# A step's score maxima turned into eight rows a head by one matmul, copied once by ACT and spread over the diagonal blocks by POOL, one step ahead

## The chip, the cores and the metric

The kernel runs on one core of one Trainium2 chip. The metric is the device time of one execution in microseconds. Its engines are TensorE (PE), VectorE (DVE), ScalarE (ACT), GpSimd (POOL) and SyncE (SP, which only issues transfers here). Each runs its own program in order and waits on semaphores.

## What is computed

A decoder layer on x of 8 x 128 tokens x 128 features, in fp32. Cut to what matters:

```
x = x + attn(layernorm(x))            # self-attention, 16 heads of 8; q and k pass a convolution;
                                      # scores = q.k / sqrt(8) * tau + delta, then softmax
x = x + xattn(layernorm(x), ctx, mask)# cross-attention, 16 heads of 8, keys from ctx, masked
x = x + ffn(layernorm(x))             # 64 experts, 8 of them chosen by a router, and a shared one
```

Both softmaxes are taken over 128 keys, with the row's maximum subtracted.

## The kernel before

The attention part has 16 steps: step s works on batch b = s % 8 of layer n = s // 8. The 16 heads are held as four groups g of four heads j. Partition block j (32 rows) of a "stacked" tile holds head 4g+j in column group g: high, middle and low parts of an fp32r split of its 8 features (from rows S_HI, S_MID, S_LO on), and in rows 0 and 1 of the block the constant ones (keys) or nothing (queries). `stack` on TensorE makes such tiles with selection matrices `pick`, ACT (`stacked_keys`, with the bias `ones_rows`) and DVE copy them to `kst` and `qst`.

For each step and group there are two products of scores:

- `scores(s, g)`: queries by a block-diagonal `kbd` (written by eight transfers a step from SP), tokens on the partitions. DVE's `maximum` reduces it over the keys to `rawmax`, negated. These scores serve for the maxima alone.
- `scoresT(s, g)`: `kst` by the block-diagonal `qbd`, keys on the partitions. `qbd` holds the queries and, in rows 0 and 1 of each 32-row block, high and low part of the negated maximum, so that the product already has the maximum subtracted. ACT's `exponential` reads it, `pv` multiplies by the values and a column of ones, `copy_o`, `turn_out`, `norm`, `turn_on`, `copy_on`, `project` and `add_residual` finish the batch, with the statistics of the next layer norm behind them (`stats_of`).

In the second layer each product of scores is preceded by a bf16 product that adds the mask.

How `qbd` comes about (before): DVE's `split_max(s)` writes the maxima as columns 32j and 32j+1 of a 128x4x128 tile `negmax` (one 128-column block for each g, fp32, the rest zero). TensorE's `turn_max(s)` (lines 482 to 492) puts the stacked queries into `bank[5]` by an identity product and adds four 128-column fp32 transposes of `negmax`, one for each g. Then ACT copies the 32-row blocks j = 0, 1 to the diagonal blocks of `qbd` (line 855, two instructions, `qbd_high`) and DVE j = 2, 3 (line 1098, two, `qbd_ready`).

The order of each engine's work is written out by hand in the loop over s. TensorE, plain step: `scores(s+1,0)`, `turn_max(s)`, `scores(s+1,1)`, `project(s-2)`, `pv(s-1,0)`, `pv(s-1,1)`, `scores(s+1,2)`, `pv(s-1,2)`, `pv(s-1,3)`, `scoresT(s,0)`, `scoresT(s,1)`, `scores(s+1,3)`, `turn_out(s-1)`, `scoresT(s,2)`, `scoresT(s,3)`, `turn_on(s-1)`. `later(s, place)` puts the stacking of queries and keys and the second layer's values, for which there was no time before, at places 0 to 3 of steps 0 to 5. Steps 7 and 11 (`making`) make the second layer's stacked queries and have their `scores(s+1, ...)` late in the step. ACT, plain step: the two copies, `copy_o(s-1)`, four `exponential`s, `copy_on(s-1)`. DVE: `split_max(s)`, `maximum(s+1,0)`, its two copies, `maximum(s+1,1)`, `add_residual(s-2)`, `maximum(s+1,2)`, `maximum(s+1,3)`, `norm(s-1)`.

POOL has little in the steps: it scales the first layer's values (line 1371), it runs `normalise` (lines 246 to 267: 15 linked operations on 128x4, then four of 128x128) and `add_bias` (line 272) for each half of the batches once the statistics of residuals 0 to 3 (DVE step 5) and 4 to 7 (step 9) are there, it splits the first three pairs of expert weights (lines 1398 to 1405), and then runs `normalise` for the third layer norm's first half (residual 11, step 13). The expert stage behind the attention, some 160 us, is not touched.

Of the kernel before, what the change touches and what calls it, by code (L numbers as in the profile page):

```python
# [15 lines left out]
P = 128  # L16
B = 8
# [12 lines left out]
S_HI, S_MID, S_LO = 2, 2 + DK, 2 + 2 * DK  # L30
# [26 lines left out]
def decoder_layer(nc, x, ctxT, mask, pack_a, pack_b, w3, rowsd, outT):  # L57
# [3 lines left out]
    with ExitStack() as ctx:  # L61
# [3 lines left out]
        def sem(name):  # L65
# [49 lines left out]
        negmax = sb("negmax", [P, G, P])  # L115
# [84 lines left out]
        (scored, maxed, max_split, max_turned, qbd_high, qbd_ready, scoredT, exped, pv_done, o_copied, o_turned, normed,  # L200
         on_turned, on_copied, projected, residual) = (sem(n) for n in (
             "scored", "maxed", "max_split", "max_turned", "qbd_high", "qbd_ready", "scoredT", "exped", "pv_done", "o_copied",
# [148 lines left out]
        def _(pe):  # L351
# [142 lines left out]

            def scoresT(s, g):
                n, b = s // B, s % B
                i = G * s + g
                if g == 0:
                    pe.wait_ge(qbd_high, s + 1)
# [71 lines left out]
            scores(0, 3)  # L571
            for s in range(STEPS + 1):
# [29 lines left out]
                if s >= 1:  # L602
                    pv(s - 1, 0)
                    pv(s - 1, 1)
                    if early:
                        scores(s + 1, 2)
# [4 lines left out]
                elif early:  # L611
                    scores(s + 1, 2)
# [4 lines left out]
                if early:  # L617
                    scores(s + 1, 3)
# [6 lines left out]
                if now:  # L625
                    scoresT(s, 2)
                if making is not None:
# [7 lines left out]
                if making is not None:  # L635
                    turn_out(s - 1)
                if making is not None:
# [7 lines left out]
                if 1 <= s < STEPS:  # L645
                    turn_on(s - 1)

# [97 lines left out]
        def _(act):  # L745
# [38 lines left out]
            def stacked_keys(n, c, g, b=7):  # L784
                act.wait_ge(k_stacked, G * (2 * n + c) + g + 1)
                act.activation(half(kst[n][:, g, :, :], c), four(b), ACT.Identity,
                               bias=A("ones_rows")).then_inc(kst_ready, 1)
# [105 lines left out]

            for s in range(STEPS + 1):
# [33 lines left out]
                if s >= 1:  # L928
                    copy_on(s - 1)

# [44 lines left out]
        def _(dve):  # L975
# [45 lines left out]

            for m, at in ((0, S_HI), (0, S_LO), (1, S_MID), (2, S_HI), (2, S_MID), (3, S_LO)):
# [62 lines left out]
            def split_max(s):  # L1085
                dve.wait_ge(maxed, G * s + G)
                wait(dve, max_turned, s)
                cols = negmax[:, :, :].rearrange("p g (j c) -> p g j c", j=J)
                link(dve.tensor_copy(cols[:, :, :, 0:1].bitcast(F32R), rawmax[:, s % 2, :, :].unsqueeze(3)))
                dve.tensor_tensor(cols[:, :, :, 1:2], rawmax[:, s % 2, :, :].unsqueeze(3), cols[:, :, :, 0:1],  # L1090
                                  ALU.subtract).then_inc(max_split, 1)

            def queries_with_max(s):
# [382 lines left out]
```

## Time and profile before

| what | value |
|---|---|
| time, median of 3 runs | 351.7 us (349.95 to 353.64) |
| span of the profiled execution | 351.6 us (that run's own time 353.76) |
| PE busy | 321.5 us (91%) |
| DVE busy | 273.0 us (78%) |
| ACT busy | 219.1 us (62%) |
| POOL busy | 171.6 us (49%) |
| share of PE in the chain that ended last | 63% |

Busy time counts a matmul from its start to its modelled end, so overlapping matmuls show an engine as full that still waits a little. The granted clock is TensorE's, in tenths of full speed on the page and as a fraction elsewhere. A row "x2" in a timeline is two like instructions one after the other, and the bracket behind a row is the idle time before it with what ended it. The span runs from 0; the attention steps lie between 50 and 175 us.

### The profile page before, as it was taken

Reading aid. Unit: us, or ns where it says so; the run is one execution under the profiler, and the core shown is the slowest. Engines: PE = TensorE matmul, PEld = TensorE weight load, DVE = VectorE, ACT = ScalarE, POOL = GpSimd, SP = SyncE. Lnnn points to the kernel's source line nnn. Section 1 sums busy time; section 2 is a strip of 40 time slices with the busy share of each in tenths; the row PEclk is TensorE's granted clock in tenths of the full one; section 3 lists DMA queues with packets and bytes.
Section 4 is the critical chain, followed back from the end, with each engine's and each line's share of the span. In section 5 each row is a group of like instructions: output and inputs, shape, how many; then the busy total and the mean of one; then the engine's idle time right before and its main releaser. Section 6 shows DMA issues by size and latency. Waiting matters only on the chain.

```text
span 351.6 us, 6529 instructions
## 1 busy us (share of the span) xinstructions
PE 321.5 (91%) x1874; PEld 225.4 (64%) x1874; DVE 273.0 (78%) x580; ACT 219.1 (62%) x457; POOL 171.6 (49%) x247
## 2 busy tenths in 40 slices
PE   1799978999999999999965999799989999999995
PEld 1544855777666676666753676566667777777773
DVE  4997766678886777787798969999996666777664
ACT  1287724866786457456744696567667676667763
POOL 9430010000080039107148787677777677777772
PEclk9999966999999999999998999999999999999999
DMA  7600110121120121121000123133223233222201
GB/s 289 209 1 0 23 31 7 32 61 32 30 50 16 39 53 33 23 51 56 2 2 0 30 71 103 47 90 89 74 66 97 81 90 90 80 82 86 67 1 62
DMA packets 20971, 20.58 MB, mean 59 GB/s; under 512 B 3152, under 2 KB 20304, under 8 KB 20816
## 3 DMA queue, kind: packets, MB, share of 16 engines
q1 hardware_dynamic: 20944, 20.25, 21.0%
q8 instruction: 13, 0.21, 0.3%
q14 instruction: 14, 0.11, 0.1%
HBM read 15.78 MB, written 0.52 MB: 46 GB/s over the span
## 4 chain that ended last, share of the span: by engine, by line
PE 63%; DVE 13%; POOL 11%; issue 9%; ACT 2%; DMA 1%; POOLq 0%; ACTq 0%; DVEq 0%
PE bank L356 41%; POOL qbd L1418 7%; PE bank L491 5%; PE bank L731 3%; PE bank L733 3%; PE bank L732 3%; PE bank L716 2%; PE bank L504 2%; PE bank L478 2%; POOL kst L1393 2%; DVE rawmax L1082 1%; DMA xres<-x 1%; PE bank L522 1%; DVE qbd L1098 1%; POOL xn L266 1%
## 5 line engine op out<-in xcount | busy, mean ns | idle before, releaser
L356 PE MATMUL bank<-khl,kst 128*128 128x512 f32 x396 | 105.2, 401 | 3.4 <-DVE kst L1119 3.0
L1418 POOL TENSOR_TENSOR qbd<-vs,qbd 128x512 fp32r<-128x512 f32 x65 | 85.3, 1314 | 38.6 <-ACT qbd L965 38.5
L356 PEld LDWEIGHTS bank<-khl,kst 128*128 128x128 f32 x396 | 74.0, 190 | 23.4 <-DVE kst L1119 5.9
L1302 DVE TENSOR_TENSOR conv<-qin,bank 128x512 f32<-128x512 f32 x66 | 45.2, 685 | 29.1 <-PE bank L356 23.2
L936 ACT ACTIVATE qin<-bank 128x512 f32<-128x512 f32 x66 | 39.3, 598 | 33.5 <-PE bank L356 33.4
L1082 DVE TENSOR_REDUCE rawmax<-bank 128x4 f32<-128x512 f32 x64 | 43.0, 683 | 15.3 <-PE bank L356 14.9
L965 ACT ACTIVATE qbd<-vs 128x512 fp32r<-128x512 f32 x66 | 41.3, 626 | 15.2 <-DVE vs L1319 15.2
L1319 DVE TENSOR_TENSOR vs<-conv,bank 128x512 f32<-128x512 f32 x64 | 43.4, 678 | 0.5 <-PE bank L716 0.5
L252 POOL TENSOR_SCALAR nwt<-mv 128x4 f32<-128x4 f32 x4 | 0.9, 230 | 77.6 <-DVE mv L980 77.6
L731 PE MATMUL bank<-qbd,kst 128*128 128x512 f32 x66 | 37.4, 567 | 1.2 <-POOL qbd L1418 0.7
L846 ACT ACTIVATE conv<-bank 128x512 f32<-128x512 f32 x64 | 35.0, 596 | 5.8 <-PE bank L356 5.2
L356 PE MATMUL bank<-kbd,qst 128*128 128x512 f32 x64 | 34.3, 544 | 0.4 <-DVE rawmax L1082 0.4
L1119 DVE TENSOR_TENSOR kst<-ring,kst 128x256 fp32r<-128x256 f32 x63 | 33.8, 536 | 0.0
L855 ACT ACTIVATE qbd<-bank 32x512 fp32r<-32x512 f32 x32 | 18.8, 588 | 23.2 <-PE bank L491 23.0
L1393 POOL TENSOR_TENSOR kst<-ring,kst 128x128 fp32r<-128x128 f32 x64 | 33.1, 517 | 0.2
L1098 DVE CAST qbd<-bank 32x512 fp32r<-32x512 f32 x32 | 22.2, 693 | 11.7 <-PE bank L491 11.5
L356 PE MATMUL bank<-qbd,kst 128*128 128x512 f32 x64 | 30.1, 521 | 0.3
L733 PE MATMUL bank<-qbd,kst 128*128 128x512 f32 x66 | 26.1, 395 | 0.0
L873 ACT ACTIVATE kst<-ring 128x256 fp32r<-128x256 f32 x63 | 25.7, 409 | 0.0
L732 PE MATMUL bank<-qbd,kst 128*128 128x512 f32 x66 | 25.7, 389 | 0.0
L716 PE MATMUL bank<-conv 128*128 128x512 f16 x64 | 25.2, 397 | 0.0
L491 PE MATMUL bank<-pa,negmax 128*128 128x128 f32 x128 | 18.2, 287 | 3.7 <-DVE negmax L1090 3.5
(189 smaller groups left out, 552.5 us busy)
## 6 DMA issues: line engine op xcount, KB each, us to landing
ring<-w SPq DMA_DIRECT2D x66, 192.0 KB, 2.4
kbd<-kst SPq DMA_DIRECT2D x60, 64.0 KB, 2.0
pa<-pack_a SPq DMA_DIRECT2D x1, 1140.0 KB, 6.5
xres<-x SPq DMA_DIRECT2D x1, 512.0 KB, 4.2
ctxs<-ctxT SPq DMA_DIRECT2D x1, 512.0 KB, 7.1
outT<-qc SPq DMA_DIRECT2D x2, 256.0 KB, 2.0
pb<-pack_b SPq DMA_DIRECT2D x1, 449.0 KB, 7.9
masku<-mask SPq DMA_DIRECT2D x1, 128.0 KB, 7.9
```

The source lines that it names most:

```text
L356: return pe.matmul(out, lhsT, rhs, start=start, stop=stop)
L491: last = pe.matmul(bank[5][:, P * g:P * g + P], negmax[:, g, :], ident, start=False, stop=(g == G - 1), skip_group_check=True)
L731: pe.matmul(acc, whid[:, w, :], hhi[:, w, :], start=False, stop=False, skip_group_check=True)
L732: pe.matmul(acc, whid[:, w, :], hlo[:, w, :], start=False, stop=False, skip_group_check=True)
L733: pe.matmul(acc, wlod[:, w, :], hhi[:, w, :], start=False, stop=stop, skip_group_check=True).then_inc(down_done, 1)
L936: act.activation(sg[:, 4 * p:4 * p + 4, :], four(2 + p), ACT.Silu).then_inc(silu_done, 1)
L965: act.activation(hhi[:, k % 4, :].rearrange("p (b t) -> p b t", b=4), hx[k % 4], ACT.Copy).then_inc(hhi_ready, 1)
L1082: dve.tensor_reduce(rawmax[:, s % 2, g, :].unsqueeze(2), bank[i % 2][:, :].rearrange("p (j k) -> p j k", j=J), AX.X, ALU.max, negate=True) ...
L1302: dve.tensor_tensor(gu[:, 4 * p:4 * p + 4, :], sg[:, 4 * p:4 * p + 4, :], four(4 + p), ALU.mult)\
L1319: dve.tensor_tensor(hx[k % 4], gu[:, 4 * p:4 * p + 4, :], four(6 + p), ALU.mult).then_inc(h_done, 1)
L1393: pool.tensor_tensor(wlod[:, k % 4, :], ring[:, k % RING, 2, :], whid[:, k % 4, :].bitcast(F32), ALU.subtract).then_inc(wlod_ready, 1)
L1418: pool.tensor_tensor(hlo[:, k % 4, :].rearrange("p (b t) -> p b t", b=4), hx[k % 4], hhi[:, k % 4, :].bitcast(F32).rearrange("p (b t) -> p ...
```

## The change

The eight rows 0 to 7 of each 32-row block now carry the maxima: rows 2m and 2m+1 high and low part for group m, for all four groups in one 128x128 tile `negmax`. S_HI, S_MID and S_LO move up by six rows. Keys of group g have ones only in rows 2g and 2g+1 of each block (`key_rows`, made once on DVE), so each group takes its own. `turn_max` adds one 512-column fp32r product in place of four 128-column fp32 ones. Its result goes by one ACT copy of 128x512 to `qmax` (the tile `qin`, free by then; two halves), and POOL's new `queries(s)` copies it in four instructions of 32x512 to the diagonal blocks of `qbd`. `turn_max`, the ACT copy, `split_max` and `queries` are made for step s+1 during step s. Some of the `scores(s+1, ...)` move to other places in TensorE's order. POOL's program gets the calls of `queries` between its other work.

```diff
-S_HI, S_MID, S_LO = 2, 2 + DK, 2 + 2 * DK
+S_HI, S_MID, S_LO = 2 * G, 2 * G + DK, 2 * G + 2 * DK
...
# TensorE, turn_max
-                wait(pe, qbd_high, s)
-                wait(pe, qbd_ready, s)
+                wait(pe, max_copied, s)
...
                 pe.wait_ge(max_split, s + 1)
-                for g in range(G):
-                    last = pe.matmul(bank[5][:, P * g:P * g + P], negmax[:, g, :], ident, start=False,
-                                     stop=(g == G - 1), skip_group_check=True)
-                last.then_inc(max_turned, 1)
+                pe.matmul(bank[5][:, :].rearrange("p (g t) -> p g t", g=G), negmax[:, :],
+                          identr[:, :].unsqueeze(1).broadcast_to([P, G, P]), start=False, stop=True,
+                          skip_group_check=True).then_inc(max_turned, 1)
...
# TensorE, loop over s
+            turn_max(0)
             for s in range(STEPS + 1):
...
                 if early:
                     scores(s + 1, 0)
-                if now:
-                    turn_max(s)
-                if early:
-                    scores(s + 1, 1)
                 later(s, 0)
...
                 if s >= 1:
                     pv(s - 1, 0)
+                if early:
+                    scores(s + 1, 1)
+                if s >= 1:
                     pv(s - 1, 1)
-                    if early:
-                        scores(s + 1, 2)
+                if early:
+                    scores(s + 1, 2)
+                if s >= 1:
                     pv(s - 1, 2)
                     pv(s - 1, 3)
...
+                if early:
+                    scores(s + 1, 3)
                 later(s, 1)
                 if now:
                     scoresT(s, 0)
                     scoresT(s, 1)
-                if early:
-                    scores(s + 1, 3)
...
                 if now:
                     scoresT(s, 2)
+                if early:
+                    turn_max(s + 1)
...
                     turn_on(s - 1)
+                if making is not None:
+                    turn_max(s + 1)
...
# ACT
             def queries_with_max(s):
                 act.wait_ge(max_turned, s + 1)
-                wait(act, scoredT, G * (s - 1))
-                for j in range(2):
-                    r = slice(32 * j, 32 * j + 32)
-                    last = act.activation(qbd[r, s % 2, :, j, :], bank[5][r, :].rearrange("p (g t) -> p g t", g=G),
-                                          ACT.Copy)
-                last.then_inc(qbd_high, 1)
+                wait(act, qbd_ready, s - 1)
+                act.activation(qmax[:, 512 * (s % 2):512 * (s % 2) + 512].bitcast(F32R), bank[5][:, :], ACT.Copy)\
+                    .then_inc(max_copied, 1)
...
                     exponential(s, 2)
                 if making is not None:
                     second_stacked(making, 2)
+                elif s + 1 < STEPS:
+                    queries_with_max(s + 1)
                 if s < STEPS:
                     exponential(s, 3)
...
                     copy_on(s - 1)
+                if making is not None:
+                    queries_with_max(s + 1)
...
# DVE: its queries_with_max is gone
-                if s < STEPS:
-                    split_max(s)
                 if early:
                     maximum(s + 1, 0)
-                if s < STEPS:
-                    queries_with_max(s)
-                if early:
                     maximum(s + 1, 1)
...
                 if early:
                     maximum(s + 1, 2)
                     maximum(s + 1, 3)
+                    split_max(s + 1)
...
# POOL
+            def queries(s):
+                pool.wait_ge(max_copied, s + 1)
+                wait(pool, scoredT, G * (s - 1))
+                src = qmax[:, 512 * (s % 2):512 * (s % 2) + 512].rearrange("p (g t) -> p g t", g=G)
+                for j in range(J):
+                    r = slice(32 * j, 32 * j + 32)
+                    last = pool.tensor_copy(qbd[r, s % 2, :, j, :], src[r, :, :])
+                last.then_inc(qbd_ready, 1)
+                pool.wait_ge(qbd_ready, s + 1)
...
+            queries(0)
             pool.wait_ge(delta_ready, 2)
             pool.wait_ge(v_copied, 2)
...
-            for c in range(2):
-                normalise(pool, link, 1, 4 * c, 4 * c + 4, False)
-                add_bias(pool, Bw("bo"), 4 * c, 4 * c + 4, B + 4 * c + 4)
+            for s in range(1, 10):
+                queries(s)
+                if s in (5, 9):
+                    c = s // 8
+                    normalise(pool, link, 1, 4 * c, 4 * c + 4, False)
+                    add_bias(pool, Bw("bo"), 4 * c, 4 * c + 4, B + 4 * c + 4)
+                    pool.wait_ge(bias_added, 2 + c)
...
+            queries(10)
             pool.wait_ge(exped, G * B)
             for k in range(LAG):
+                wait(pool, wlod_ready, k)
+                queries(11 + k)
                 pool.wait_ge(ld_w[k], 16)
...
             normalise(pool, link, 2, 0, 4, False)
+            pool.wait_ge(xn_ready, 2 * B + 4)
+            queries(14)
+            queries(15)
             low_inputs(0)
```

## Rows read from the trace of the kernel before

**Rows 1.** Busy time by stretch: start:end, length, busy (instructions) per engine, granted clock, DMA share, GB/s

```profile
151.10:165.10 14.00, 14.00 (x134) 9.31 (x130) 10.89 (x27) 8.09 (x16) 5.05 (x18) 1.00 0.24 63
```

**Rows 2.** Timeline of step 13 (second layer): start us, length us, engine, line, operation, tiles

```profile
158.06 0.39 PE L504 MATMUL bank<-identb,maskb 128*128 128x512 bf16 x1
...
158.72 1.09 ACT L846 ACTIVATE conv<-bank 128x512 f32<-128x512 f32 x2
...
160.52 1.09 ACT L846 ACTIVATE conv<-bank 128x512 f32<-128x512 f32 x2 [0.72 <-PE bank L356]
...
160.74 0.17 DVE L1089 CAST negmax<-rawmax 128x16 fp32r<-128x16 f32 x1
...
161.50 0.28 ACT L840 ACTIVATE onT<-bank 128x128 f32<-128x128 f32 x1
...
161.74 1.05 PE L491 MATMUL bank<-pa,negmax 128*128 128x128 f32 x8
...
162.63 0.38 PE L478 MATMUL bank<-maskb,identb 128*128 128x512 bf16 x1
...
163.08 0.38 PE L356 MATMUL bank<-pb,onT 128*128 128x128 f32 x2
...
165.06 0.39 PE L504 MATMUL bank<-identb,maskb 128*128 128x512 bf16 x1
```

**Rows 3.** Timeline of step 5 (first layer), TensorE, ACT and POOL

```profile
95.68 0.73 PE L356 MATMUL bank<-qbd,kst 128*128 128x512 f32 x2
...
96.38 0.23 POOL L252 TENSOR_SCALAR nwt<-mv 128x4 f32<-128x4 f32 x1 [33.67 <-DVE mv L980]
...
98.48 0.68 ACT L786 ACTIVATE kst<-bank,pa 128x512 fp32r<-128x512 f32 x1
...
99.96 0.38 PE L356 MATMUL bank<-pa,onT 128*128 128x128 f32 x2
...
101.81 0.73 PE L356 MATMUL bank<-qbd,kst 128*128 128x512 f32 x2
...
104.00 1.09 POOL L272 TENSOR_TENSOR xres<-xres,pb 128x512 f32<-128x512 f32 x1
```

**Rows 4.** Groups by form, 40 to 200 us: busy, mean ns, idle before

```profile
L1098 DVE CAST qbd<-bank 32x512 fp32r<-32x512 f32 x32 | 22.2, 693 | 11.7 <-PE bank L491 11.5
...
L834 ACT ACTIVATE oT<-bank 128x512 f32<-128x512 f32 x16 | 9.6, 599 | 15.0 <-PE bank L356 15.0
```

**Rows 5.** Groups by form on POOL over the span

```profile
L1418 POOL TENSOR_TENSOR qbd<-vs,qbd 128x512 fp32r<-128x512 f32 x65 | 85.3, 1314 | 38.6 <-ACT qbd L965 38.5
L1393 POOL TENSOR_TENSOR kst<-ring,kst 128x128 fp32r<-128x128 f32 x64 | 33.1, 517 | 0.2
...
L1402 POOL TENSOR_TENSOR kst<-ring,kst 128x256 fp32r<-128x256 f32 x3 | 2.2, 748 | 0.2
...
L1400 POOL CAST kst<-ring 128x256 fp32r<-128x256 f32 x3 | 1.2, 398 | 0.0
...
L1404 POOL CAST kst<-ring 128x128 fp32r<-128x128 f32 x3 | 0.9, 290 | 0.0
```

**Rows 6.** Timeline around the first step's maxima

```profile
51.39 2.17 POOL L1371 TENSOR_TENSOR vs<-vs,edelta 128x1152 f32<-128x1152 f32 x1 [30.77 <-DVE vs L1036]
...
51.82 1.78 DVE L1089 CAST negmax<-rawmax 128x16 fp32r<-128x16 f32 x1
...
53.88 2.08 PE L491 MATMUL bank<-pa,negmax 128*128 128x128 f32 x8 [3.17 <-DVE negmax L1090]
```

**Rows 7.** Busy time by stretch around two long waits of TensorE

```profile
50.60:53.90 3.30, 0.13 (x2) 0.03 (x1) 3.08 (x8) 0.00 (x0) 2.17 (x1) 0.87 0.39 80
...
184.60:188.70 4.10, 0.29 (x5) 0.24 (x4) 3.82 (x18) 0.00 (x0) 3.03 (x13) 1.00 0.00 0
...
189.80:193.00 3.20, 3.20 (x9) 2.16 (x8) 2.69 (x6) 2.26 (x6) 3.20 (x5) 0.50 0.00 0
53.90:59.60 5.70, 5.44 (x16) 4.24 (x17) 3.19 (x5) 2.19 (x4) 0.00 (x0) 0.50 0.00 0
```

More of the change, by code:

```diff
@@ L114, in decoder_layer @@
         rawmax = sb("rawmax", [P, 2, G, J])
-        negmax = sb("negmax", [P, G, P])
+        negmax = sb("negmax", [P, P], F32R)
+        key_rows = sb("key_rows", [P, G])
+        qmax = qin[:, :, :].rearrange("p b t -> p (b t)")
         on = sb("on", [P, H, DK])
@@ L199, in decoder_layer @@
         const_ready = sem("const_ready")
-        (scored, maxed, max_split, max_turned, qbd_high, qbd_ready, scoredT, exped, pv_done, o_copied, o_turned, normed,
+        (scored, maxed, max_split, max_turned, max_copied, qbd_ready, scoredT, exped, pv_done, o_copied, o_turned, normed,
          on_turned, on_copied, projected, residual) = (sem(n) for n in (
-             "scored", "maxed", "max_split", "max_turned", "qbd_high", "qbd_ready", "scoredT", "exped", "pv_done", "o_copied",
+             "scored", "maxed", "max_split", "max_turned", "max_copied", "qbd_ready", "scoredT", "exped", "pv_done", "o_copied",
              "o_turned", "normed", "on_turned", "on_copied", "projected", "residual"))
@@ L498, in scoresT @@
                 if g == 0:
-                    pe.wait_ge(qbd_high, s + 1)
                     pe.wait_ge(qbd_ready, s + 1)
@@ L610, in _ @@
                         project(s - 2)
-                elif early:
-                    scores(s + 1, 2)
+                if early:
+                    scores(s + 1, 3)
                 later(s, 1)
@@ L634, in _ @@
                     second_stack(making, 3)
-                if making is not None:
                     turn_out(s - 1)
-                if making is not None:
                     scores(s + 1, 2)
@@ L786, in stacked_keys @@
                 act.activation(half(kst[n][:, g, :, :], c), four(b), ACT.Identity,
-                               bias=A("ones_rows")).then_inc(kst_ready, 1)
+                               bias=key_rows[:, g:g + 1]).then_inc(kst_ready, 1)
             act.wait_ge(ld_a, 16)
@@ L892, in later @@
                     later_stacked(*LATER[PLACES.index((s, place))])
+            queries_with_max(0)
             for s in range(STEPS + 1):
                 inputs, making = {6: 0, 10: 1}.get(s), {7: 0, 11: 1}.get(s)
-                if s < STEPS:
-                    queries_with_max(s)
                 later(s, 0)
@@ L1020, in _ @@
             later_taps(1, "del1")
+            dve.tensor_reduce(key_rows[:, :].unsqueeze(2).unsqueeze(3),
+                              ident.rearrange("p (j m c) -> p m j c", j=J, c=2)[:, 0:G, :, :], AX.XY, ALU.add)\
+                .then_inc(dve_step, 1)
+            steps[0] += 1
             for m, at in ((0, S_HI), (0, S_LO), (1, S_MID), (2, S_HI), (2, S_MID), (3, S_LO)):
@@ L1087, in split_max @@
                 wait(dve, max_turned, s)
[L1088 to L1093, printed above, removed]
-                dve.wait_ge(max_turned, s + 1)
-                wait(dve, scoredT, G * (s - 1))
-                for j in range(2, J):
-                    r = slice(32 * j, 32 * j + 32)
-                    last = dve.tensor_copy(qbd[r, s % 2, :, j, :], bank[5][r, :].rearrange("p (g t) -> p g t", g=G))
-                last.then_inc(qbd_ready, 1)
+                cols = negmax[:, :].rearrange("p (j m c) -> p m j c", j=J, c=2)[:, 0:G, :, :]
+                link(dve.tensor_copy(cols[:, :, :, 0:1], rawmax[:, s % 2, :, :].unsqueeze(3)))
+                dve.tensor_tensor(cols[:, :, :, 1:2], rawmax[:, s % 2, :, :].unsqueeze(3),
+                                  cols[:, :, :, 0:1].bitcast(F32), ALU.subtract).then_inc(max_split, 1)
             def norm(s):
@@ L1244, in _ @@
             dve.memset(bank[4][:, :], 0.0).then_inc(bank4_zeroed, 1)
+            split_max(0)
             for s in range(STEPS + 1):
@@ L1287, in _ @@
                     maximum(s + 1, 3)
+                    split_max(s + 1)
             compare_groups(0)
@@ L1353, in _ @@
                 pool.memset(v[:, :, :, DK:DK + 1], 1.0).then_inc(ones_ready, 1)
-            pool.memset(negmax[:, :, :], 0.0).then_inc(ones_ready, 1)
+            pool.memset(negmax[:, :].bitcast(F32), 0.0).then_inc(ones_ready, 1)
             pool.memset(qbd[:, :, :, :, :].bitcast(F32), 0.0).then_inc(rows_ready, 1)
@@ L1366, in _ @@
             link, steps = chain(pool, pool_step)
+            def queries(s):
[7 more added lines that the diff above has]
+                pool.wait_ge(qbd_ready, s + 1)
+            pool.wait_ge(rows_ready, 3)
+            pool.wait_ge(mask_ready, 1)
+            pool.wait_ge(bias_added, 1)
+            queries(0)
             pool.wait_ge(delta_ready, 2)
```

6 lines of the change are left out of this document (1 added, 5 removed).

## The prediction

> **What bounds the kernel now.** I read the page's busy times first, then busy times by stretch, then the timeline of one step of each attention layer, then the groups by form for prices, and last the timeline and the granted clock at the start. TensorE is busy without a gap through the second layer's plain steps, while DVE has 10.89 of 14.0 us, ACT 8.09 and POOL 5.05 [rows 1]. That is where work can be moved to. But "busy" there is pipelined, so I go through one step by the clock.
>
> I name by T(s) the moment at which TensorE starts the first `scoresT` of step s. T(13) is 158.06 and T(14) 165.06, so a step of the second layer is 7.00 us [rows 2]. In the first layer T(5) is 95.68 and T(6) 101.81, or 6.13 us [rows 3]. Inside step 13 the reader is to see these offsets from T: first exponential +0.66, third exponential +2.46, `copy_on` +3.44, the four maxima matmuls +3.68 to +4.57, `project` +5.02, next T +7.00 [rows 2]. So `project` has 1.3 us of room behind `copy_on` today, and the maxima matmuls lie in that room.
>
> **TensorE's saving.** Four fp32 128-column products (eight records) take 0.89 us from first start to the next instruction's start (161.74 to 162.63). The one 512-column product that replaces them should take what a 512-column fp32r product with its mask partner shows, half of 162.63 to 163.08, 0.23 us [rows 2]. That is 0.66 us a step. If TensorE alone were the bound, a second-layer step would be 6.34 us.
>
> **What waits instead.** ACT copies the turned maxima between the third and the fourth exponential, and `copy_on`, for which `project` waits, is last in ACT's step. A step in the new order, second layer: `scores(s+1,3)` now lies ahead of T, so what follows T comes 0.45 us earlier: third exponential at +2.0 to +2.55 (half of the pair's 1.09), the copy of 128x512 at 0.60 [rows 2, 4] to +3.15, fourth exponential to +3.7, `copy_on` 0.28 to +4.0, `project` at +4.05. From `project` to the next T is 1.98 us today (163.08 to 165.06), with one block of scores in it; the new order has three, so two more of 0.45 make 2.88. Next T: +6.9. The gain is 0.1 us a step, not 0.66: TensorE would stand idle for some 0.6 us ahead of `project`. I take 0.1, and keep 0.66 as the other end.
>
> The same for the first layer: exponentials from +0.42 in 0.55 each [rows 2], the third from +1.52, the copy to +2.7, the fourth to +3.3, `copy_on` to +3.6, or 4.3 where a stacked-keys copy of 0.68 lies between (98.48, steps 0 to 5), then `project` to next T 1.85 (99.96 to 101.81) plus two blocks of 0.23 [rows 3]. That is 6.0 or 6.65 against 6.13: steps 1 to 5 gain nothing. In T(6) to T(7) I allow 0.5. Steps 7 and 11 end with wait for the maxima, split, turn, as today; DVE's 1.40 there (2 copies of 0.69 [rows 4]) becomes 0.6 + 2.5 on ACT and POOL, but the turn is made before `scores(s+2,0)`, and 3.3 us of TensorE work (scores, `project`, `pv`) lies beside it: nothing either way. All this gives 1.0 us in the stage (0 to 8 at the full 0.66).
>
> **POOL's new price.** Four copies of 32x512 a step. No row has the shape. DVE's 32x512 copy takes 0.69, no less than ACT's 128x512 of 0.60 [rows 4], so I count free elements, not partitions. POOL's casts take 398 ns for 256 and 290 ns for 128 elements, 0.84 ns for each further one: 614 ns for 512, 2.46 us for four. Below, 4 x 0.29 = 1.2 us; above, 4 x 1.31 = 5.3 us, the two-input 128x512 row [rows 5]. One input and one cast are nearest to the casts: 2.45. From the end of the ACT copy at +3.15 to +5.7: in a plain step hidden until +6.9.
>
> **Where it is not hidden.** POOL works in order, and its own program sets `normalise` between `queries(5)` and `queries(6)`, between `queries(9)` and `queries(10)`, and, behind three blocks of weight splitting, between `queries(13)` and `queries(14)`. `normalise` waits for residual 3, 7, 11, which DVE adds in step 5, 9, 13. So it starts at about T+0.3 (today 96.38 = T(5)+0.7; DVE reaches it earlier without its copies) and lasts, with `add_bias`, from 96.38 to 105.09, 8.7 us [rows 3]. The queries of the next step stand behind it, `scoresT(s+1,0)` waits for them, and everything on TensorE behind that waits too. Nothing covers it: the scores of step s+2 and `pv` of step s are by then done.
> - T(6) = T(5) + 0.3 + 8.7 + 2.45 + 0.1 = T(5) + 11.55, against 6.13: 5.4 lost.
> - T(10) = T(9) + 0.0 + 8.7 + 2.55 = T(9) + 11.25 (second layer: `project` lies further ahead of T, so normalise starts nearer T), against 7.0: 4.25 lost.
> - T(14): `queries(13)` ends at T(13) - 1.2, the third weight block is 0.40 + 0.75 + 0.29 + 0.52 = 1.96 [rows 5], so `normalise` starts at +0.8, without `add_bias` it is 7.6, then 2.55: T(13) + 10.95, against 7.0: 3.95 lost.
>
> Sum 13.6 us.
>
> **The clock.** After 3.3 us in which TensorE had 0.13 of work the next 5.7 us ran at a granted clock of 0.50, and after 4.1 us with 0.29 of work came 3.2 us at 0.50 [rows 7]. The three new waits of 4 to 5 us are of that size. In 3.2 us at half the clock 1.6 us of product time is lost, in 5.7 us 2.85, some of it beside ACT. I take 1.5 each, 4.4 in all; 0 to 8 as ends. The Trainium skill says so too ("TensorE: Matmul & The Clock Gate", HAM oscillation): waits between bursts put the clock back to its lower level and the next burst starts cold. By that rule every new wait would pay; by the rows alone two such waits of two did; the sum is the same.
>
> **The start.** Today DVE's first split needs 1.78 us for a cast of 16 elements, 51.82 to 53.60, and ends when POOL's 51.39 + 2.17 = 53.56 ends; TensorE waits for it 3.2 us [rows 6]. In the new order POOL scales the values after `queries(0)`, so the cast takes its usual 0.17 (160.74) [rows 2] and the first turn is 1.6 us earlier. Then 0.6 + 2.45 replaces DVE's 1.40, beside scores of step 1; ACT, freed of 1.2 us, stacks earlier. Between 0 and 3.3, I take 2.5. The Trainium skill ("SBUF — State Buffer", two separate sides) calls this a lock: DVE and POOL share one port pair, and whichever starts first keeps it for the whole instruction. The trace agrees (1.78 against 0.17). It also speaks against the change: 64 new POOL copies can each hold the split's cast. By the order above the split falls at T+0.9 and the copies end before T, so this costs nothing unless the copies run late; by the rule in every step it would cost up to 0.6 x 16 = 9.6 us.
> The router's DVE chain behind step 15 gains some 0.4, since `project` there stands behind two more ACT copies and not behind DVE's.
>
> **Sum** against the profiled execution's span of 351.6 (the median of the runs is 351.7, so the two are one): 351.6 - 2.5 - 1.0 - 0.4 + 13.6 + 4.4 = 365.7, said as 365.5.
>
> **Rivals.**
> - *No clock loss.* The three waits are there, TensorE's clock stays up (only two stretches of the trace speak against it). 361.3. Chance 0.17.
> - *TensorE gains fully.* `copy_on` comes in time, 12 unstalled steps give 0.66 each, 7.9 instead of 1.0. 358.8, or 354.4 without clock loss. For it: TensorE's record has no gaps. Against it: ACT's order above. Chance 0.12 together, with a quarter of it within 1%.
> - *DVE's cycle was the bound* (the one on the other side). If each of the 12 unstalled steps is shortened by DVE's whole 1.40 us, that is 16.8; 351.6 - 2.5 - 16.8 - 0.4 + 13.6 = 345.5. It decides from 1.2 us a step on (the 13.6 and 3.5 for 1%, less 2.9, by 12). Against it: DVE has 3 of 14 us free [rows 1]. Chance 0.05.
> - *The copies or the lock gate every step.* At 1.0 us a copy POOL ends at +7.2 instead of +5.7, so five second-layer steps are 0.3 longer, seven first-layer steps about 0.5, and each stall 1.55: 365.7 + 1.5 + 3.5 + 4.7 = 375.4. With the lock in each step, 375.3. Chance 0.08.
> - *It hides after all*: the waits are absent, for instance because `normalise` runs in half its time. Then 351.6 - 3.9 = 347.7. Against it: 96.38 to 105.09 is one chain of POOL alone, with no wait in it to lose [rows 3]. Chance 0.02.
>
> **How the numbers follow.** The forecast keeps 0.56. It and the first two rivals make 0.85; with 356 to 373 I leave out the low end of the second, the dear copies and the faster cases, nearly 0.2. A measurement here tells about 1% from no change, that is 348.2 to 355.2. Faster 0.06, within 1% 0.07, slower 0.87.
>
> **What the profile of after would show.** Right: three waits of TensorE at `scoresT` released by POOL, of 4 to 5 us, near 95 to 105, 130 to 140 and 165 to 175; 128x4 links just before them; dips of the granted clock behind them; POOL copies at 0.6; step starts of the second layer some 6.9 apart and a wait for ACT's `copy_on` ahead of `project`; DVE's first split at 0.2. Wrong: second-layer steps at 6.3 (the `project` reading fails); copies at 1 us or more (their price fails); `queries(6)` ahead of `normalise` in POOL's order (the waits fail).

## The result and the profile after

| | before | after |
|---|---|---|
| time, median | 351.3 us | 373.4 us (371.5 to 375.1) |
| ratio, 95% interval | 1 | 1.062 [1.054, 1.070] |
| span of the profiled execution | 351.6 | 373.0 |
| ACT busy, POOL busy | 219.1, 171.6 | 210.3, 210.1 |
| DVE busy | 273.0 | 251.9 |

The change makes the kernel 22 us slower. The prediction said 365.5 with 356 to 373: the direction and its mechanism came true, the size was two thirds of what came, and the time lies just outside the range. The largest part that it missed is a loss in the first layer's steps.

The page after (busy time and share; the granted clock in 40 slices; a group by line):

```profile
span 373.0 us, 6315 instructions
...
PE 322.3 (86%) x1762; PEld 217.4 (58%) x1762; DVE 251.9 (68%) x549; ACT 210.3 (56%) x441; POOL 210.1 (56%) x311
...
PEclk9899779999979997999988799989999999999999
...
L1369 POOL CAST qbd<-qin 32x512 fp32r<-32x512 f32 x64 | 39.0, 610 | 94.8 <-issue 52.6
```

The clock has dips in slices 12, 16 and 21 (from 103, 140 and 187 us on) where before, in its steps, it had none. A 32x512 copy of POOL takes 610 ns, against the 614 worked out from [rows 5].

TensorE's waits between 50 and 195 us (what waited, for what, and then us in total, how many times, the longest):

```profile
PE bank L503 <- POOL qbd L1369: 8.0, 2, 4.1
PE bank L491 <- DVE negmax L1094: 5.2, 4, 2.7
PE bank L358 <- POOL qbd L1369: 4.5, 1, 4.5
PE bank L358 <- ACT kst L786: 4.2, 6, 1.0
PE bank L358 <- ACT onT L840: 2.3, 5, 0.9
```

Three waits for POOL, 12.5 us together; then the waits for DVE's split, and eleven for ACT's stacked keys and `copy_on` that the kernel before did not have.

Start of the first `scoresT` of each step, T(s), read from the timelines of both, and the time to the next:

| s | T before | step | T after | step | after less before |
|---|---|---|---|---|---|
| 0 | 58.94 | 7.27 | 56.07 | 8.40 | -2.87 |
| 1 | 66.21 | 8.23 | 64.47 | 8.74 | -1.74 |
| 2 | 74.44 | 7.92 | 73.21 | 8.46 | -1.23 |
| 3 | 82.36 | 6.74 | 81.67 | 7.46 | -0.69 |
| 4 | 89.10 | 6.58 | 89.13 | 7.13 | +0.03 |
| 5 | 95.68 | 6.13 | 96.26 | **11.50** | +0.58 |
| 6 | 101.81 | 6.76 | 107.76 | 7.76 | +5.95 |
| 7 | 108.57 | 10.85 | 115.52 | 11.33 | +6.95 |
| 8 | 119.42 | 6.99 | 126.85 | 7.03 | +7.43 |
| 9 | 126.41 | 6.98 | 133.88 | **11.25** | +7.47 |
| 10 | 133.39 | 6.58 | 145.13 | 9.07 | +11.74 |
| 11 | 139.97 | 11.11 | 154.20 | 11.62 | +14.23 |
| 12 | 151.08 | 6.98 | 165.82 | 7.02 | +14.74 |
| 13 | 158.06 | 7.00 | 172.84 | **11.15** | +14.78 |
| 14 | 165.06 | 6.89 | 183.99 | 8.42 | +18.93 |
| 15 | 171.95 | to the end 179.65 | 192.41 | to the end 180.59 | +20.46 |

So the loss came in three jumps (steps 5, 9 and 13 are 5.37 + 4.27 + 4.15 = 13.8 us longer than before's), in the step behind each jump, and in a creep through the first layer.

Step 9 after, TensorE, ACT and POOL (start, length, engine, line). It answers to [rows 2], of which the same offsets were taken:

```profile
133.88 0.39 PE L503 MATMUL bank<-identb,maskb 128*128 128x512 bf16 x1
...
135.88 0.60 ACT L846 ACTIVATE conv<-bank 128x512 f32<-128x512 f32 x1 [0.26 <-PE bank L358]
...
136.38 0.59 ACT L853 ACTIVATE qin<-bank 128x512 fp32r<-128x512 f32 x1
...
137.33 0.30 ACT L840 ACTIVATE onT<-bank 128x128 f32<-128x128 f32 x1
...
137.68 0.49 PE L358 MATMUL bank<-pb,onT 128*128 128x128 f32 x2 [0.36 <-ACT onT L840]
...
138.07 3.15 POOL L268 TENSOR_SCALAR xn<-xres,mv,nwt 128x128 f32<-128x128 f32 x4
...
141.30 1.09 POOL L274 TENSOR_TENSOR xres<-xres,pb 128x512 f32<-128x512 f32 x1
...
142.46 2.62 POOL L1369 CAST qbd<-qin 32x512 fp32r<-32x512 f32 x4
...
145.13 0.61 PE L503 MATMUL bank<-identb,maskb 128*128 128x512 bf16 x1 [4.07 <-POOL qbd L1369]
```

Third exponential +2.00, the new copy +2.50, `copy_on` +3.45, `project` +3.80 behind a wait of 0.36 for it; then POOL's four scalings to 141.2, `add_bias` to 142.4, the four copies at 142.46 to 145.08, and TensorE idle for 4.07 us until 145.13 = T(9) + 11.25.

### The profile page after: what moved, and what is told of

It is laid out like the page before. It is cut to its first block, busy times and chain, and to the rows that moved or that the text cites. A ratio compares the mean times of both kernels' runs of the same rounds, so it can differ in the third digit from the quotient of the medians.

```text
span 373.0 us, 6315 instructions
## 1 busy us (share of the span) xinstructions
PE 322.3 (86%) x1762; PEld 217.4 (58%) x1762; DVE 251.9 (68%) x549; ACT 210.3 (56%) x441; POOL 210.1 (56%) x311
## 4 chain that ended last, share of the span: by engine, by line
PE 28%; POOL 11%; issue 6%; DVE 4%; ACT 1%; POOLq 0%; DVEq 0%; ACTq 0%
PE bank L358 17%; POOL qbd L1435 6%; PE bank L731 3%; PE bank L733 3%; PE bank L732 3%; PE bank L716 2%; POOL kst L1404 2%; POOL xn L268 1%; DVE kin L1159 1%; DVE conv L1296 1%; DVE vs L1313 1%; POOL qbd L1369 0%; DVE tauT L1142 0%; PE bank L503 0%; ACT qbd L965 0%
## 5 line engine op out<-in xcount | busy, mean ns | idle before, releaser
L1369 POOL CAST qbd<-qin 32x512 fp32r<-32x512 f32 x64 | 39.0, 610 | 94.8 <-issue 52.6
L358 PEld LDWEIGHTS bank<-khl,kst 128*128 128x128 f32 x396 | 75.0, 192 | 22.3 <-DVE kst L1115 5.0
L846 ACT ACTIVATE conv<-bank 128x512 f32<-128x512 f32 x64 | 36.6, 599 | 22.1 <-PE bank L358 21.5
L731 PE MATMUL bank<-qbd,kst 128*128 128x512 f32 x66 | 37.9, 574 | 1.4 <-POOL qbd L1435 0.9
L358 PE MATMUL bank<-qbd,kst 128*128 128x512 f32 x64 | 33.2, 556 | 5.2 <-POOL qbd L1369 4.5
L1115 DVE TENSOR_TENSOR kst<-ring,kst 128x256 fp32r<-128x256 f32 x63 | 32.3, 513 | 0.0
L834 ACT ACTIVATE oT<-bank 128x512 f32<-128x512 f32 x16 | 9.6, 598 | 33.8 <-PE bank L358 33.8
L733 PE MATMUL bank<-qbd,kst 128*128 128x512 f32 x66 | 26.3, 398 | 0.0
L732 PE MATMUL bank<-qbd,kst 128*128 128x512 f32 x66 | 25.9, 393 | 0.0
L358 PE MATMUL bank<-conv,vs 128*9 128x128 f32 x512 | 21.5, 274 | 0.0
L503 PE MATMUL bank<-identb,maskb 128*128 128x512 bf16 x32 | 13.9, 434 | 8.0 <-POOL qbd L1369 8.0
```

The lines of the kernel that those rows point to most:

```text
L358: return pe.matmul(out, lhsT, rhs, start=start, stop=stop)
L731: pe.matmul(acc, whid[:, w, :], hhi[:, w, :], start=False, stop=False, skip_group_check=True)
L732: pe.matmul(acc, whid[:, w, :], hlo[:, w, :], start=False, stop=False, skip_group_check=True)
L733: pe.matmul(acc, wlod[:, w, :], hhi[:, w, :], start=False, stop=stop, skip_group_check=True).then_inc(down_done, 1)
L1369: last = pool.tensor_copy(qbd[r, s % 2, :, j, :], src[r, :, :])
```

## Experiments

All times are beside runs of the kernel before on the same chip; ratios are to those. The nine kernels (one of them run twice) are compared by T(s) as well. Executions of one kernel differ by up to 5 us (351.8 to 356.4 for the first below). The one kernel that has two traces (one matmul) differs by 2.1 us in T(0), by 0.1 from T(0) to T(15) and by 0.9 from there to the end, so T(s) says more on single steps than the medians do.

### POOL's order alone

The chain of small links of `normalise` (scale=False) runs in the step in which the whole of it ran, and its four scalings (`normalised`) go behind the next step's copies. `add_bias` goes behind the copies of steps 7 and 11, and the third block of weight splitting behind those of step 15.

```diff
-            for s in range(1, 10):
+            for s in range(1, 11):
                 queries(s)
                 if s in (5, 9):
-                    normalise(...); add_bias(...); pool.wait_ge(bias_added, 2 + c)
+                    normalise(..., scale=False)
+                if s in (6, 10):
+                    normalised(...)
+                if s == 7:
+                    add_bias(...); pool.wait_ge(bias_added, 2)
...
+            queries(11)
+            add_bias(...); pool.wait_ge(bias_added, 3)
...
             queries(13)
-            normalise(pool, link, 2, 0, 4, False)
+            normalise(pool, link, 2, 0, 4, False, scale=False)
             queries(14)
+            normalised(pool, 2, 0, 4)
             queries(15)
+            weights(2)
```

> The changed kernel with POOL's order alone mended: normalise is cut in two (its 15 small links, and its four scalings with add_bias), and the queries of steps 6, 10 and 14 stand between the halves instead of behind both; the third block of weight splitting goes behind the queries of step 15. Theory 1 (the three blocked steps and the low clock behind them make 13.8 + 5 of the 21 us that the change cost): T(5) to T(6), T(9) to T(10) and T(13) to T(14) fall from 11.5, 11.25 and 11.15 us to 7 to 7.7, the granted clock stays at 1.00 between 57 us and the router, and the time falls from 373 to 355, between 352 and 359. Rival 2 (ACT's order in every plain step is the loss, POOL is not): at most 3 us fall, to 370. Rival 3 (POOL's copies gate all steps, since POOL has the same work in sum): 365 to 368.

Measured: 354.5 us, ratio 1.0055 [1.0012, 1.0099]. T(5) to T(6), T(9) to T(10), T(13) to T(14) are 6.99, 7.03 and 7.02; the steps behind them 6.54, 6.40 and 6.92. The granted clock is 1.00 from 57 to 174 us. Theory 1 holds to half a microsecond, and the rivals' 365 to 370 are out: 19 of the 22 us are the three places in POOL's program, with what follows on the clock.

### TensorE busy in the wait

```diff
                 if g == 0:
+                    if s in (6, 10, 14):
+                        for _ in range(16):
+                            pe.matmul(bank[7][:, :]..., identr[:, :], identr..., start=True, stop=True)
                     pe.wait_ge(qbd_ready, s + 1)
```

> The changed kernel with 16 products of the identity by itself, 512 columns each, into the free bank 7 ahead of the blocked scoresT of steps 6, 10 and 14, where TensorE waits 4.0 to 4.5 us for POOL. Their result is overwritten. They change nothing but what TensorE does in the wait. Theory of the clock: the granted clock stays at 1.00 through steps 6 to 8, 10 to 12 and 14 to 15, T(10) to T(11) falls from 9.07 to 7 or below, T(6) to T(7) from 7.76 to 6.5, T(14) to T(15) from 8.4 to 7, and the time falls by 4 to 5.5 us to 368. If the low clock costs nothing (the steps behind a wait being bound by ACT), it stays at 373 within 1.

Measured: 368.0 us, ratio 1.0448 [1.0384, 1.0513], 5.4 us less than the changed kernel. In the two fences, first the changed kernel's busy time by stretch, for each of the first two waits and the stretch behind it and the one behind the third wait (start:end, length, busy per engine, granted clock, DMA share, GB/s), then the same of the kernel with the fill, in and behind the second wait:

```profile
105.20:107.70 2.50, 0.00 (x0) 0.00 (x0) 0.08 (x1) 0.00 (x0) 2.37 (x4) 0.79 0.40 79
107.70:112.50 4.80, 4.74 (x15) 3.66 (x15) 0.55 (x2) 2.83 (x6) 0.61 (x2) 0.50 0.00 0
141.00:145.10 4.10, 0.06 (x1) 0.00 (x0) 1.58 (x4) 0.17 (x1) 3.80 (x6) 0.89 0.32 65
145.10:151.20 6.10, 6.07 (x19) 4.10 (x19) 0.55 (x2) 2.99 (x5) 0.70 (x2) 0.52 0.02 5
184.00:188.50 4.50, 4.50 (x16) 3.07 (x17) 0.55 (x2) 2.44 (x5) 0.32 (x1) 0.63 0.01 4
```

```profile
137.00:140.00 3.00, 2.94 (x13) 2.06 (x11) 1.24 (x2) 0.00 (x0) 2.80 (x5) 1.00 0.34 72
140.00:147.00 7.00, 6.05 (x57) 4.00 (x57) 1.27 (x4) 4.21 (x9) 3.36 (x7) 1.00 0.04 9
```

In the changed kernel the clock is at its lower level, 0.50 (1.2 GHz), as soon as TensorE starts again, for some 5, 6 and 3 us; filled, it stays at 1.00. The blocked steps themselves take as long (11.48, 11.19, 11.13), and the steps behind them fall from 7.76, 9.07, 8.42 to 6.11, 6.39, 6.91: 5.8 us, which is the clock's share.

```profile
136.80 3.14 PE L501 MATMUL bank<-identr 128*128 128x512 f32 x13
140.27 0.39 PE L507 MATMUL bank<-identb,maskb 128*128 128x512 bf16 x1 [0.33 <-POOL qbd L1373]
```

This is TensorE's timeline of the second fill (cut at 140 us): the products end, and `scoresT` still waits for POOL, in the three places 0.84, 0.33 and 0.27 us. So the products take the place of idleness alone.

### TensorE's order alone

The line moved behind `pv(s - 1, 1)` holds for steps 1 to 5, the first layer's.

```diff
                 if early:
                     scores(s + 1, 0)
-                later(s, 0)
...
-                if s >= 2 and now:
-                    project(s - 2)
...
                     pv(s - 1, 1)
+                    later(s, 0)
+                if s >= 2 and now:
+                    project(s - 2)
                 if early:
                     scores(s + 1, 2)
```

> The changed kernel with TensorE's order alone mended in steps 1 to 15: the later stacks of place 0 and project(s-2) are moved from ahead of pv(s-1,0) to behind pv(s-1,1), so that what needs no ACT copy is done while ACT makes its last two. Theory 1 with its second part (in a plain step TensorE waits some 0.4 to 0.9 us for ACT's stacked keys and copy_on, because the copy of the turned maxima and the fourth exponential now stand ahead of them): steps 1 to 4 fall from 8.7, 8.5, 7.5 and 7.1 by 0.5 to 0.8 each, plain second-layer steps from 7.03 by 0.4, the three blocked steps by less than 0.3 since POOL ends them; in all 3 to 5 us, 368 to 370. If TensorE's own work is the bound of these steps, nothing changes (373).

Measured: 369.9 us, ratio 1.0487 [1.0432, 1.0542]. Steps 0 to 4 take 7.29, 7.42, 7.36, 6.48, 6.13 (after: 8.40, 8.74, 8.46, 7.46, 7.13), plain second-layer steps 6.50. That is 5.5 us regained in steps 0 to 4 and 1.1 in steps 8 and 12. The median falls by 3.5 only: the blocked steps stay (11.35, 11.02, 11.67), and step 14, behind the last, grows from 8.42 to 9.83. The 3.5 us are within the 3 to 5 expected, but not step by step: steps 1 to 4 fell by 1.0 to 1.3 us each (0.5 to 0.8 expected), and step 13 grew by 0.5.

### Both orders

The two edits above together.

> Both mended orders together: POOL's (queries ahead of the second half of normalise) and TensorE's (place 0 and project behind pv(s-1,1)). If the two losses are separate and add, steps 1 to 5 take 7.3, 7.4, 7.4, 6.5, 6.1 as with TensorE's order alone, steps 6, 10 and 14 take no more than the plain 6.5, and the time is that with POOL's order alone (354.5) less 5 + 2.6: 346.5 to 348. If POOL's copies become the bound as soon as TensorE's order is mended, plain steps end by POOL and it stays at 352 to 354.

Measured: 348.7 us, ratio 0.990 [0.987, 0.993]. Steps 0 to 4 are 7.20, 7.41, 7.36, 6.47, 6.12, plain ones 6.50 to 6.59, so the two losses are separate. The time is 0.7 us above the range expected: steps 6, 10 and 14 take 6.88, 6.85 and 7.33 where POOL's order alone had 6.54, 6.40 and 6.92, which I had not expected. TensorE's waits (57 to 190 us) for POOL and for the stacked keys that are left:

```profile
PE bank L364 <- POOL qbd L1377: 1.1, 1, 1.1
...
PE bank L364 <- ACT kst L794: 0.3, 1, 0.3
```

### One half of TensorE's order each

Only `project` moved, and only place 0 moved, both on top of POOL's mended order.

> POOL's mended order, and of TensorE's order only project(s-2) moved behind pv(s-1,1). The place-0 work of steps 1 to 5 stays ahead of pv(s-1,0). If project's wait for copy_on is what the second layer's plain steps lose, they fall from 7.03 to 6.5; steps 1 to 5, where place 0 waits for the stacked keys before project is reached, keep more than half of their excess (8.7, 8.5, 7.5, 7.1 fall by 0.3 at most). In all 354.5 less 3.5 to 4.5: 350 to 351.

> POOL's mended order, and of TensorE's order only the place-0 work of steps 1 to 5 moved behind pv(s-1,1). Then the second layer stays at 7.03, and steps 1 to 5 fall by 0.5 to 1.0 each if the wait for ACT's stacked keys (4.2 us in six waits in the changed kernel) is their loss: 354.5 less 3 to 4.5, 350 to 351.5. If that wait only hides project's, steps 1 to 5 stay within 0.2 of 8.7, 8.5, 7.5, 7.1 and the time at 354.

Measured: 355.5 us (1.007 [1.002, 1.012]) and 354.4 us (1.004 [1.000, 1.009]): neither gains anything over 354.5. With `project` alone, plain second-layer steps fall to 6.50 as expected, but steps 6, 10 and 14 grow by 0.35 to 0.45, step 0 takes 9.09 instead of 8.21, and the first layer keeps 8.65, 8.36, 7.47, 7.13, with its waits for the stacked keys (TensorE's waits, us in total, times, longest):

```profile
PE bank L364 <- ACT kst L792: 3.6, 5, 1.0
```

With place 0 alone the second layer stays at 7.03, as expected, and the first layer stays at 8.8, 8.55, 7.6 and 7.3, against my expectation: the wait for the keys is gone and `project` waits for `copy_on` in its place.

```profile
74.41 0.30 ACT L848 ACTIVATE onT<-bank 128x128 f32<-128x128 f32 x1
...
74.76 0.49 PE L364 MATMUL bank<-pa,onT 128*128 128x128 f32 x2 [0.90 <-ACT onT L848]
```

The keys' copy and `copy_on` are neighbours at the end of ACT's step (76.62 and 77.20 in the changed kernel), so taking one wait away leaves the other, 0.9 us long. In the first layer only both moves together free the step.

### ACT's copy last

```diff
-                elif s + 1 < STEPS:
-                    queries_with_max(s + 1)
                 if s < STEPS:
                     exponential(s, 3)
...
                     copy_on(s - 1)
-                if making is not None:
+                if s + 1 < STEPS:
                     queries_with_max(s + 1)
```

> The changed kernel with ACT's copy of the turned maxima moved from between the third and fourth exponential to the end of ACT's step, behind the stacked keys and copy_on. If ACT's order is what TensorE waits for in plain steps, second-layer plain steps fall from 7.03 to 6.65 (then ended by POOL, whose copies start 0.9 later), steps 1 to 5 by 0.3 to 0.9 each; the three blocked steps stay at 11.2 to 11.5; in all 369.5 to 371. If the wait was TensorE's own work, plain steps stay at 7.03 or grow, since POOL starts later: 373 to 377.

Measured: 374.5 us, ratio 1.063 [1.058, 1.069]: a miss. Plain second-layer steps stay at 6.99. From ACT and TensorE in step 8, T(8) = 124.04:

```profile
126.98 0.60 ACT L846 ACTIVATE conv<-bank 128x512 f32<-128x512 f32 x1 [0.34 <-PE bank L358]
127.48 0.27 ACT L840 ACTIVATE onT<-bank 128x128 f32<-128x128 f32 x1
...
127.64 0.60 ACT L853 ACTIVATE qin<-bank 128x512 fp32r<-128x512 f32 x1
...
127.80 0.49 PE L358 MATMUL bank<-pa,onT 128*128 128x128 f32 x2 [0.30 <-ACT onT L840]
```

`copy_on` is at +3.44 and `project` at +3.76, where the changed kernel has +3.45 and +3.80. The copy cost `copy_on` almost nothing in the second layer: it had lain in time in which ACT waits for the fourth `scoresT` anyway (0.34 us of that wait are left here). In the first layer steps 0 to 4 fell by 1.1, 0.5, 0.3, 0.2 and 0.1, and steps 13 and 14 grew by 1.1 and 1.5. What brings `project` into the wait is TensorE's order, with one block of scores between `turn_on` and `project` instead of the turn and two.

### One matmul in the order of before

The kernel before with the eight rows, `key_rows` and the one product of `turn_max`; the copies by ACT and DVE, and every order, as before.

```diff
-                for g in range(G):
-                    last = pe.matmul(bank[5][:, P * g:P * g + P], negmax[:, g, :], ident, ...)
+                pe.matmul(bank[5][:, :]..., negmax[:, :], identr[:, :].unsqueeze(1).broadcast_to([P, G, P]), ...)
```

> The kernel before with one part of the change alone: eight rows of maxima a block, key_rows, and one 512-column fp32r product in turn_max in place of four fp32 ones of 128 columns. Copies to qbd by ACT and DVE, the order of all engines and the step in which things are made stay as before. Theory: in the order of before nothing waits on ACT ahead of project, so TensorE's 0.66 us a step comes through in second-layer steps (7.00 to 6.35) and half of it in first-layer steps; 16 steps give 7 to 10 us, 342 to 344.5. Rival: the saving is taken up by a wait for DVE's chain of maxima and copies, which is as long; 349 to 351.

Measured: 344.7 us, ratio 0.975 [0.968, 0.983], and on a second chip:

> The one matmul alone once more, on the same chip as the run with the later scaling, so that the two can be compared: 342 to 346 as before.

342.9 us, 0.974 [0.970, 0.979]. Plain second-layer steps take 6.33 to 6.37 us, as TensorE's saving of 0.66 says. Two rows of TensorE in step 9 (T(9) = 126.56, the next T at 132.93):

```profile
130.31 0.49 PE L491 MATMUL bank<-identr,negmax 128*128 128x512 f32 x1
...
131.62 0.38 PE L357 MATMUL bank<-pb,onT 128*128 128x128 f32 x2
```

`project` starts at +5.06 and waits for nothing. So the new product is worth 7.7 and 9.1 us in the two measurements, and the changed kernel gave all of it away by what it was built in with.

### One matmul, values scaled after the first split

```diff
             pool.wait_ge(v_copied, 2)
+            pool.wait_ge(max_split, 1)
```

> One matmul in the order of before, and POOL's scaling of the first layer's values waits for the first split. Theory (the cast of the first split waits for POOL's running instruction, in the kernel before 1.78 us instead of 0.17): that cast takes 0.17 to 0.2 us, the first turn comes 1.6 us earlier and the whole is 0.5 to 1.6 us faster than one matmul alone. If the cast is slow for another reason, it stays at 1.8 and nothing moves.

Measured: 341.0 us (340.2 to 342.7), ratio 0.970 [0.967, 0.973], against 0.974 [0.970, 0.979] for one matmul alone on the same chip: 1.9 us between the medians, with intervals that still touch. The start of both, one matmul alone first (POOL's scaling, DVE's cast, the turn):

```profile
49.00 2.17 POOL L1375 TENSOR_TENSOR vs<-vs,edelta 128x1152 f32<-128x1152 f32 x1 [28.87 <-DVE vs L1040]
...
49.43 1.78 DVE L1093 CAST negmax<-rawmax 128x16 fp32r<-128x16 f32 x1
...
51.49 0.79 PE L491 MATMUL bank<-identr,negmax 128*128 128x512 f32 x1 [3.18 <-DVE negmax L1094]
```

```profile
48.66 0.50 PE L491 MATMUL bank<-identr,negmax 128*128 128x512 f32 x1 [1.56 <-DVE negmax L1094]
...
48.78 2.18 POOL L1376 TENSOR_TENSOR vs<-vs,edelta 128x1152 f32<-128x1152 f32 x1 [28.46 <-DVE negmax L1094]
```

In the first the cast ends at 51.21, the scaling at 51.17. In the second no cast lies beside it: the cast takes 0.17 us (48.21) and the turn comes 2.8 us earlier. In these traces T(0) is 52.08 against 55.27, more than the 1.6 us that the cast gives, and T(0) to T(15) is the same (105.8). But the clock differs too: with one matmul alone it is 0.50 between 44 and 46 us, with the later scaling 1.00 there. So the fast cast is shown, and how much of the 1.9 us (0.5 to 1.6 expected) it gives is not. This is the fastest kernel here, 3% below the one before.

## Why the prediction was right and wrong

**Right: the three blocked steps.** T(6) - T(5), T(10) - T(9), T(14) - T(13) were forecast as 11.55, 11.25 and 10.95 and measured as 11.50, 11.25 and 11.15; lost 13.8 against 13.6. POOL in step 5, with the same chain as [rows 3]:

```profile
96.26 0.63 PE L358 MATMUL bank<-qbd,kst 128*128 128x512 f32 x2
96.31 0.23 POOL L254 TENSOR_SCALAR nwt<-mv 128x4 f32<-128x4 f32 x1 [1.79 <-DVE mv L980]
...
103.93 1.09 POOL L274 TENSOR_TENSOR xres<-xres,pb 128x512 f32<-128x512 f32 x1
104.18 0.88 DVE L1093 CAST negmax<-rawmax 128x16 fp32r<-128x16 f32 x1
105.09 2.61 POOL L1369 CAST qbd<-qin 32x512 fp32r<-32x512 f32 x4
...
107.76 0.80 PE L358 MATMUL bank<-qbd,kst 128*128 128x512 f32 x1 [4.50 <-POOL qbd L1369]
```

`normalise` begins at 96.31, T(5) + 0.05, not T(5) + 0.3, `add_bias` ends at 105.02, the four copies take 2.61 (2.45 forecast), `scoresT` follows at 107.76. The first and the third of these differences nearly cancel. POOL's order alone removes the waits, so this is shown.

**Right in kind, 1.4 short: the clock.** Forecast 4.4, measured 5.8 by the filled waits (1.65, 2.68 and 1.50; 1.5 each forecast). All three waits paid, and the lower level held for some 5, 6 and 3 us behind them, the lengths of the two stretches of [rows 7].

**Right: the price of the copies** (610 against 614 ns), and that in plain steps they are hidden: no wait of TensorE for POOL but the three.

**Wrong: "steps 1 to 5 gain nothing", and with it the 1.0 us gained in the stage.** T(0) to T(5) grew by 3.45 us. The sentence followed ACT's chain to `copy_on` and had `project` as the only thing that waits for it. What it left out is named in the same sentence: the stacked-keys copy of 0.68. TensorE's place 0 of the next step waits for that copy, stands ahead of `project`, and has 0.6 to 1.0 us of its own products. ACT and TensorE at the end of step 2 and in step 3 of the changed kernel (T(2) = 73.21):

```profile
75.67 0.59 ACT L853 ACTIVATE qin<-bank 128x512 fp32r<-128x512 f32 x1
...
76.62 0.70 ACT L786 ACTIVATE kst<-bank,key_rows 128x512 fp32r<-128x512 f32 x1
...
77.20 0.30 ACT L840 ACTIVATE onT<-bank 128x128 f32<-128x128 f32 x1
...
77.38 1.16 PE L358 MATMUL bank<-pb,ctxs 128*128 128x128 f32 x8 [0.74 <-ACT kst L786]
...
78.37 0.39 PE L358 MATMUL bank<-pa,onT 128*128 128x128 f32 x2
```

The turned maxima are copied at 75.67, the keys at 76.62, and only at 77.38 do the values' products of place 0 start, behind a wait of 0.74. `project` has to queue behind them, to 78.37 (T(2) + 5.16, where the forecast has it behind a `copy_on` that ends at +4.3), and `pv` behind that. The forecast has no term for place 0 between ACT's chain and `project`. TensorE's order regains the loss (5.5 us of steps 0 to 4), each half of it alone does not.

**Wrong in size: steps 7 and 11.** Forecast 0 each, measured +0.48 and +0.51 against before. With both orders mended they still take 11.45 and 11.7, and with one matmul in the old order 10.2 and 10.5. The forecast weighed ACT and POOL's 3.1 us against DVE's 1.40, and took them as covered. They were, by very little. In step 7 after, the turn and POOL's copies:

```profile
122.94 0.49 PE L491 MATMUL bank<-identr,negmax 128*128 128x512 f32 x1 [1.06 <-DVE negmax L1094]
...
124.19 2.56 POOL L1369 CAST qbd<-qin 32x512 fp32r<-32x512 f32 x4 [9.75 <-issue]
```

and before, the first product of `scores(9,0)` and the turn behind it:

```profile
115.05 0.38 PE L478 MATMUL bank<-maskb,identb 128*128 128x512 bf16 x1 [0.36 <-DVE rawmax L1082]
...
116.00 1.16 PE L491 MATMUL bank<-pa,negmax 128*128 128x128 f32 x8
```

The turn starts at T(7) + 7.42, as before (+7.43). But `scores(9,0)`, which before filled part of the time until DVE's split, now stands behind the turn, and TensorE waits 1.06 us for the split. From the turn to T(8) it takes 3.91 us, against 3.42, without a wait. The copies end at 126.75. T(8), at 126.85, follows 0.47 us behind the start of TensorE's last block of scores (126.38), as T(9) follows 0.46 behind its own, so TensorE's own order ends the step and not POOL. The trace thus points to the moved block; no run moves it by itself.

**Half right: the second layer's plain steps.** 7.03 and 7.02 against 6.9, so the saving of 0.66 was indeed lost, and only in part for the reason given. The wait for `copy_on` is there, but 0.36 us long and not 0.6: `copy_on` starts at +3.45, where it stood before (+3.44), and not at +3.7, since the copy, the fourth exponential and `copy_on` start 0.48 us apart and not 0.6 and 0.55, and `project` comes at +3.80, not +4.05. From there to the next T it took 3.2, not 2.88, with `pv` and scores changing places three times more; that these changes cost the rest was not tried by itself. ACT's copy last changed neither. What loses the saving is TensorE's order: moving `project` gives 6.50.

**The start** gave -2.87 at T(0), against 2.5; but in the changed kernel the slow cast is still there, one step later (56.52, 1.79 us, beside the scaling at 56.09), and T(0) of two kernels with the same start was 52.88 and 56.07, by where the low clock fell. So it is partly luck that this term came out near.

**The end.** Forecast -0.4, measured +0.95 from T(15). The other kernels built on the changed one lie between 180.0 and 181.7 there, so the blocked steps are not its cause. Up to POOL's first product of the expert stage (213.48, before 192.90) it is 21.07 against 20.95, so the 0.4 that the router should have gained did not come. The other 0.8 lies in the expert stage, which the change does not touch: 159.5 against 158.7. The granted clock there is 0.83 in one stretch of 10 us (243.5 to 253.5), where before has 1.00 throughout; the kernel with both orders has 1.00 too, and takes 159.1. What brings that dip stays open.

Of the 7.3 us between 365.7 and 373.0, 3.5 are steps 0 to 4, 1.2 the other plain and making steps, 1.4 the clock, 1.3 the end, 0.2 the blocked steps, and -0.4 the start. The range failed since I gave ACT's chain in the first layer one end only: what it would cost if more than `project` waited for it was not in the bounds.

The rival *TensorE gains fully* is the truth of another kernel: with its old order. The rivals on DVE's cycle and on dear copies did not occur. Nor did the lock in every step: no cast of the split lay beside one of POOL's new copies.

## What to carry to other kernels

When work is moved to an engine with time to spare, write down that engine's whole program around it: POOL had 9 of 14 us free, but two of its three new calls in question stood behind a chain of 8.7 us and the third behind one of 7.6, and TensorE waited for them. When an instruction is inserted into an engine's step, look for everything that waits for what stands behind it, not for the first such waiter; two waits on neighbours took each other's place here, and mending one of them gained nothing in those steps. A saving should be tried without its surroundings first: the new product alone was worth 2.5%, the whole change cost 6%.

## What the runs showed of the hardware

- A copy of 32 partitions by 512 elements took POOL 610 ns, against 614 worked out from its casts of 128 partitions by 256 and 128 elements (398 and 290 ns). On ACT 32x512 took 588 ns and 128x512 599. So the free elements set the time, and partitions that were not used saved nothing.
- A DVE cast of 16 elements took 1.78 us beside POOL's scaling of 2.17 (1.79 in the changed kernel), and in the changed kernel 0.88 at 104.18 and 0.60 at 141.83 beside `add_bias` and 0.28 at 166.74 beside a weight split, each time to within 0.05 us of the end of POOL's instruction; elsewhere it took 0.17 to 0.19. The Trainium skill ("SBUF — State Buffer", two separate sides) says that the port pair is held for the whole instruction; the trace agrees.
- 16 products of no use in each wait of TensorE kept the granted clock at 1.00 and made the kernel 5.4 us faster. The Trainium skill ("TensorE: Matmul & The Clock Gate", HAM oscillation) says that waits between bursts cost the clock; the runs agree, with 1.5 to 2.7 us for each.
- Between executions of kernels with the same instructions at the start, T(0) differed by 3 us (52.88 and 56.07), by where the low clock fell: in the slower one the granted clock was 0.50 from 42 to 48 us and 0.51 from 52 to 54, in the faster one 1.00 there, and 0.56 to 0.59 from 48 to 52.
